# A cleared scratch row behind every gather on GpSimd, in a group convolution and deformable bottleneck for sixteen images

## The chip, the cores and the metric

The kernel runs on one core of one Trainium2 chip. The metric is the device time of one execution in microseconds (us), from the first to the last instruction and the little that lies around them. Its engines are TensorE (PE in the profile, with its weight loads as PEld), VectorE (DVE), ScalarE (ACT), GpSimd (POOL) and SyncE (SP, which only issues DMAs here).

## The reference

The input is 16 images of 512 channels and 32 x 32 pixels. `_gn` is a group norm with 32 groups of 16 channels. Two residual blocks follow each other:

```python
x = x + _L0_conv_ref(_gn(x), W, b)      # 3x3 convolution in 8 groups of 64 channels, then a
                                        # transpose of (64, 1024) to (1024, 64) read as 64 channels
x = x + _L1_conv_ref(_gn(x), ...)       # bottleneck:
    out = relu(bn(conv1x1(x)))                        # 512 -> 128 channels
    offset = conv3x3(out)                             # 18 channels: dy, dx of 9 taps
    out = deform_conv3x3(out, offset)                 # 9 taps, bilinear values at y + dy, x + dx
    out = relu(bn(conv1x1(bn(out))))                  # 128 -> 512 channels
```

A tap's value is `v00*wy0*wx0 + v01*wy0*wx1 + v10*wy1*wx0 + v11*wy1*wx1`, with `v00` to `v11` taken at four neighbouring pixels whose place depends on the data.

## The kernel before, in words

For the deformable convolution each image has a table in HBM of 1152 rows (padded pixels) of 512 float32: the 128 channels of h and of its differences in x, in y and in both. With one row of 2048 bytes a bilinear value is two multiply-adds. TensorE makes the table in nine tiles of 128 rows (`table_tile`, L868), ScalarE copies them out (L447), and SP stores them (L306). VectorE turns the offsets into row numbers `ridx` and fractions `frac` (`coordinates`, L675 to L702).

An image's deformable work is cut into 18 chunks: two halves of 512 pixels by 9 taps. A chunk is four gathers (`PER = 4`) of 128 rows each. GpSimd issues each as an indirect DMA (L335) into one of 12 row buffers, three chunks deep (`RING = 3`). VectorE waits for each gather by itself and combines its rows, first in y (L570, four a chunk), then in x (L578, four a chunk, into `val`). TensorE transposes `val` (`transpose_values`, L751), ScalarE copies the result out (L363), and TensorE multiplies it with the tap's weights (`deform`, L760). After nine chunks follow the 1x1 convolution (`out_conv`, L767), ScalarE's relu (L374), VectorE's residual (L585) and SP's store (L311).

The order of the work is written out by hand. Every engine runs the same `step` for each image, in 18 slots; in one step three images are under way at different stages, and tables of slots (`CONV_FIRST`, `SHUFFLE`, `TABLE` and so on) say what falls where. The interpolation of chunk c lies in slot c + 7, its transposes a slot later, and the product two slots later. So chunks 11 to 17 of an image are interpolated in slots 0 to 6 of the next step. The other work of TensorE is the group convolution (L778), the shuffle products (L792), the 1x1 convolution into the bottleneck (L846) and the offset convolution (L811), all for later images; in the last two steps these fall away.

GpSimd's program has a loop of its own, without slots. For each image it waits for the coordinates and the table's stores. Then for each chunk c it waits for `val_done` of chunk c - 3, which frees the row buffers (L329), and issues two gathers. Before the third it waits for `valT_done` of chunk c - 3, the transposes on TensorE (L333); this is the tie that the change's title speaks of. No buffer needs it, since the first wait has freed the rows. GpSimd's only other work is four casts of weights at the start (L344).

Of the kernel before, what the change touches and what calls it, by code (L numbers as in the profile page):

```python
# [5 lines left out]
def build_program(nc, x, w_group, b_group, w_in, w_off, b_off, w_def, w_out, bn, eye, fold, blocks, offset_fold,  # L6
# [16 lines left out]
    f32, f16, i32, u32 = mybir.dt.float32, mybir.dt.float16, mybir.dt.int32, mybir.dt.uint32  # L23
# [19 lines left out]
    CHUNKS = 2 * TAPS  # L43
# [2 lines left out]
    RING = 3  # L46
    TBUFS = 3
    PER = 4
    ROW = 4 * CH
    COLS = PIX // GIN  # L50
    XBUFS = 4
# [3 lines left out]
    with ctx:  # L55
        def sb(name, shape, dt):
            return ctx.enter_context(nc.sbuf_tensor("sb_" + name, shape, dt))

        def sem(name):
            return ctx.enter_context(nc.semaphore(name))  # L60
# [9 lines left out]
        h_split = sb("h_split", [128, 2, HPLANE], f16)  # L70
        table_sb = sb("table_sb", [128, TBUFS, ROW], f32)
        rows = sb("rows", [128, RING * PER, ROW], f32)
        val = sb("val", [128, 2, PER * CH], f32)
        valT = sb("valT", [128, 2, HALF], f32)
# [13 lines left out]
        bias_off = sb("bias_off", [128, 1], f32)  # L88
        eps_sb = sb("eps_sb", [128, 1], f32)
        warm = sb("warm", [128, 2], f32)  # L90
        bn_sb = sb("bn_sb", [128, 6, 5], f32)
        bn_s = sb("bn_s", [128, 6], f32)
        bn_t = sb("bn_t", [128, 6], f32)
# [36 lines left out]
        wo_in = sem("wo_in")  # L130
        consts_in = sem("consts_in")
        pool_passed = sem("pool_passed")
        dve_passed = sem("dve_passed")
        zeroed = sem("zeroed")
        table_loaded = sem("table_loaded")
# [43 lines left out]
        pos_done = sem("pos_done")  # L179
        gathered = [[sem(f"gathered{n}_{i}") for i in range(PER)] for n in range(RING)]  # L180
        lerp_y = sem("lerp_y")
# [13 lines left out]
        def count(per, image, n):  # L195

            total = image * per + n
            return max(total, 0) if isinstance(image, int) else total
# [119 lines left out]
        @block.gpsimd  # L318
        def _(pool):
            def step(t, u, tail, b, a2, a1):  # L320
                if not b:
                    return
                pool.wait_ge(pos_done, count(1, t, 1))
                for n in range(TBUFS):
                    pool.wait_ge(tile_stored[n], count(16 * TILES // TBUFS, t, 16 * TILES // TBUFS))
                for c in range(CHUNKS):
                    half, k = divmod(c, TAPS)

                    pool.wait_ge(val_done, count(CHUNKS, t, c - RING + 1))  # L329
                    pool.sem_inc(pool_passed, 1)  # L330
                    for i in range(PER):
                        if i == 2:
                            pool.wait_ge(valT_done, count(CHUNKS, t, c - 2))  # L333
                            pool.sem_inc(pool_passed, 1)
                        pool.indirect_dma_start(  # L335
                            out=rows[:, (c % RING) * PER + i, :], out_offset=None, in_=tables[u % 2],
                            in_offset=bass.IndirectOffsetOnAxis(
                                ap=ridx[:, u % 2, half * PER + i, k:k + 1].bitcast(u32), axis=0),
                        ).then_inc(gathered[c % RING][i], 16)


            for g in range(POOL_GROUPS, GROUPS):
                pool.wait_ge(wg_in[g // 2], 2 * 16)
                nc.gpsimd.tensor_copy(wg[:, g, :, 0:GIN], raw_wg[:, g * TAPS * GIN:(g + 1) * TAPS * GIN]  # L344
                                      .rearrange("p (k o) -> p k o", o=GIN)).then_inc(w_high, 1)

            run(pool, step)
# [640 lines left out]
```

## Time and profile before

| what | value |
|---|---|
| median of 3 runs | 2096.07 us (2092.15 to 2115.77) |
| the profiled execution | 2095.71 us |
| its span, first to last instruction | 2093.9 us |
| mean granted TensorE clock | 0.911 of full speed |
| gathers | 1152, 302.06 MB in 92160 packets |
| moved by all DMA queues | 412.98 MB, mean 197 GB/s |

The profile comes from the execution in the second line; its rows are times within the span. An engine's idle time in a row is that just before the instructions named, with what ended it: another engine, a DMA, "remote" (a releaser that the trace doesn't name) or "issue" (nothing that the profile shows).

### The profile page before, as it was taken

To read this page: it belongs to the slowest core of one execution; us is meant where nothing else is said; L and a number is where in the kernel's file an instruction comes from. 1 tells how busy PE (TensorE), PEld (TensorE's weight loads), DVE (VectorE), ACT (ScalarE), POOL (GpSimd) and SP (SyncE) were. 2 spreads that over 40 slices of the span, in tenths; PEclk is the share of its full clock that TensorE was granted. 3 is DMA by queue.
4 is the path that set the end of the run, shared out by engine and by line. 5 is a ranking of instruction groups with operands and counts; after the bars stand their busy time and mean duration, and the time that the engine had idled before them with its cause. 6 is when DMAs were issued, how large, how long until landed. Compare 5 with 4: busy or idle time off the path is not lost.

```text
span 2093.9 us, 32210 instructions
## 1 busy us (share of the span) xinstructions
PE 1759.4 (84%) x10144; PEld 975.4 (47%) x10144; DVE 1398.5 (67%) x3450; ACT 963.4 (46%) x1475; POOL 1201.4 (57%) x1160
## 2 busy tenths in 40 slices
PE   4988898988898898889889888889888889987545
PEld 2545454544545454455545444444454545444322
DVE  5447587575677758577776856758576776757654
ACT  6545454353553545454454545435454544523212
POOL 0036566555665656566566656557555556657673
PEclk9989899998999989999999999889999999999766
DMA  6055657566675756667576666657666566565764
GB/s 194 1 176 161 206 176 245 171 202 208 210 235 162 251 185 215 221 209 231 163 243 197 211 213 202 213 159 227 200 213 223 172 228 195 178 214 182 241 208 147
DMA packets 142937, 412.98 MB, mean 197 GB/s; under 512 B 24614, under 2 KB 25126, under 8 KB 142758
## 3 DMA queue, kind: packets, MB, share of 16 engines
q0 software_dynamic: 92160, 302.06, 48.1%
q1 hardware_dynamic: 50598, 108.71, 14.0%
q8 instruction: 90, 1.47, 0.3%
q14 instruction: 89, 0.73, 0.1%
HBM read 339.37 MB, written 71.30 MB: 196 GB/s over the span
## 4 chain that ended last, share of the span: by engine, by line
PE 41%; DVE 21%; another core or an unknown queue 15%; issue 12%; ACT 6%; POOL 2%; DMA 1%; SPq 1%; ACTq 0%; DVEq 0%; POOLq 0%
PE bank L778 12%; DVE sb_rows L570 8%; PE bank L760 7%; PE bank L792 6%; DVE sb_val L578 5%; PE bank L767 3%; DVE sb_split L611 3%; PE bank L751 3%; PE bank L868 3%; PE bank L846 3%; PE bank L811 2%; POOL sb_rows L335 2%; DVE sb_raw L626 2%; ACT sb_split L409 1%
## 5 line engine op out<-in xcount | busy, mean ns | idle before, releaser
L335 POOL DMA_INDIRECT sb_rows<-table,sb_ridx x1152 | 1197.0, 1039 | 851.9 <-issue 425.6
L778 PE MATMUL bank<-sb_split,sb_wg 128*128 128x512 f16 x2304 | 583.5, 400 | 43.5 <-ACT sb_conv_sb L381 31.5
L570 DVE SCALAR_TENSOR_TENSOR sb_rows<-sb_rows,sb_frac 128x256 f32<-128x256 f32 x1152 | 491.3, 479 | 107.6 <-DMA sb_rows<-table,sb_ridx 82.9
L778 PEld LDWEIGHTS bank<-sb_split,sb_wg 128*128 128x128 f16 x2304 | 225.5, 101 | 356.3 <-issue 127.5
L619 DVE TENSOR_TENSOR sb_xs<-bank,sb_xs 128x512 f32<-128x512 f32 x128 | 88.3, 690 | 416.6 <-remote 309.1
L578 DVE SCALAR_TENSOR_TENSOR sb_val<-sb_rows,sb_frac 128x128 f32<-128x128 f32 x1152 | 328.7, 347 | 54.3 <-PE bank L751 30.7
L792 PE MATMUL bank<-sb_fold_sb,sb_conv_sb 128*64 128x64 f32 x4096 | 291.8, 286 | 83.5 <-issue 69.6
L760 PE MATMUL bank<-sb_valT,sb_wd 128*128 128x512 f32 x576 | 349.0, 690 | 10.7 <-issue 9.6
L363 ACT ACTIVATE sb_valT<-bank 128x512 f32<-128x512 f32 x288 | 171.4, 595 | 362.1 <-remote 199.6
L381 ACT ACTIVATE sb_conv_sb<-bank,sb_bias 128x512 f32<-128x512 f32 x256 | 173.7, 686 | 321.1 <-PE bank L778 188.5
L792 PEld LDWEIGHTS bank<-sb_fold_sb,sb_conv_sb 128*64 128x64 f32 x4096 | 262.6, 206 | 124.2 <-issue 107.3
L751 PE MATMUL bank<-sb_eye_sb,sb_val 128*128 128x128 f32 x1152 | 193.2, 290 | 78.5 <-issue 35.6
L751 PEld LDWEIGHTS bank<-sb_eye_sb,sb_val 128*128 128x128 f32 x1152 | 147.2, 150 | 200.6 <-issue 117.6
L767 PE MATMUL bank<-sb_mid,sb_w 128*128 128x512 f32 x256 | 152.5, 681 | 41.1 <-ACT sb_res L374 27.1
L447 ACT ACTIVATE sb_table_sb<-bank 128x512 f32<-128x512 f32 x144 | 86.4, 601 | 213.6 <-PE bank L868 128.9
L611 DVE TENSOR_TENSOR sb_split<-sb_norm,sb_split 64x1024 f16<-64x1024 f32 x128 | 157.1, 1227 | 14.7 <-ACT sb_split L409 10.8
L409 ACT ACTIVATE sb_split<-sb_xs,sb_gs 64x1024 f16<-64x1024 f32 x128 | 158.1, 1236 | 1.7
L396 ACT ACTIVATE sb_norm<-sb_xs 128x1024 f32<-128x1024 f32 x128 | 134.8, 1053 | 3.9 <-DMA sb_xs<-x 2.4
L760 PEld LDWEIGHTS bank<-sb_valT,sb_wd 128*128 128x128 f32 x576 | 104.6, 209 | 53.3 <-issue 32.2
L585 DVE TENSOR_TENSOR sb_res<-sb_res,sb_xs 128x512 f32<-128x512 f32 x128 | 88.1, 689 | 49.0 <-issue 30.2
L846 PE MATMUL bank<-sb_xs,sb_w_norm 128*128 128x512 f32 x256 | 117.8, 603 | 1.1 <-ACT sb_w_norm L425 1.1
L767 PEld LDWEIGHTS bank<-sb_mid,sb_w 128*128 128x128 f32 x256 | 51.7, 212 | 124.4 <-issue 80.8
(77 smaller groups left out, 1092.4 us busy)
## 6 DMA issues: line engine op xcount, KB each, us to landing
table<-sb_table_sb SPq DMA_DIRECT2D x144, 256.0 KB
sb_xs<-x SPq DMA_DIRECT2D x64, 512.0 KB
out<-sb_res SPq DMA_DIRECT2D x128, 256.0 KB
sb_rows<-table,sb_ridx POOLq DMA_INDIRECT x1152
sb_rows<-w_group SPq DMA_DIRECT2D x8, 288.0 KB, 9.4
sb_wd<-w_def SPq DMA_DIRECT2D x1, 576.0 KB
sb_w<-w_in SPq DMA_DIRECT2D x1, 256.0 KB
sb_w<-w_out SPq DMA_DIRECT2D x1, 256.0 KB
```

The source lines that it names most:

```text
L335: pool.indirect_dma_start(out=rows[:, (c % RING) * PER + i, :], out_offset=None, in_=tables[u % 2], in_offset=bass.IndirectOffsetOnAxis(ap ...
L381: nc.scalar.activation(conv_sb[:, g % 3, half * HALF:(half + 1) * HALF], pair_ps[half][:, :], ACT.Identity, bias=bias0[:, g:g + 1]).then_i ...
L409: nc.scalar.activation(plane(split1[p, 2 * q + e, :], 1, 1, HEIGHT), xs[p, un, q, :].rearrange("p (r c) -> p r c", c=WIDTH), ACT.Identity, ...
L570: op = nc.vector.scalar_tensor_tensor(r[:, 0:2 * CH], r[:, 2 * CH:4 * CH], frac[:, parity, half * PER + i, k, 0:1], r[:, 0:2 * CH], ALU.mu ...
L578: op = nc.vector.scalar_tensor_tensor(val[:, c % 2, i * CH:(i + 1) * CH], r[:, CH:2 * CH], frac[:, parity, half * PER + i, k, 1:2], r[:, 0 ...
L611: nc.vector.tensor_tensor(plane(split1[o, 2 * q + e, :], 1, 1, HEIGHT), norm1[p, :].rearrange("p (r c) -> p r c", c=WIDTH), plane(split1[p ...
L751: op = nc.tensor.transpose(valT_ps[:, i * CH:(i + 1) * CH], val[:, c % 2, i * CH:(i + 1) * CH], eye_sb[:, :])
L760: nc.tensor.matmul(def_ps[:, :], wd[:, k * CH:(k + 1) * CH], valT[:, c % 2, :], start=k == 0, stop=k == TAPS - 1).then_inc(def_done, 1)
L767: nc.tensor.matmul(out_ps[:, :], w2[:, q * 128:(q + 1) * 128], mid[:, :], start=True, stop=True)\
L778: op = nc.tensor.matmul(pair_ps[half][:, :], wg[:, g, k, :], plane(split1[:, g, :], ky + half * HROWS, kx, HROWS), start=k == 0, stop=k == ...
L792: op = nc.tensor.matmul(shuf_ps[half][64 * e:64 * e + 64, jj * GIN:(jj + 1) * GIN], conv_sb[:, (2 * q + e) % 3, j:j + COLS * (GIN - 1) + 1 ...
L846: op = nc.tensor.matmul(pair_ps[half][:, :], w1_norm[:, q * CH:(q + 1) * CH], xs[:, (u + 1) % XBUFS, q, half * HALF:(half + 1) * HALF], st ...
```

## The change

GpSimd gets a scratch tile `spacer` of four rows of 240 float16 in each partition, which nothing reads. Behind each gather it clears one row. Before a chunk's first gather it waits until the four clears of the chunk before are done. The wait before the third gather stays.

```diff
+    SPACE = 240
...
+        spacer = sb("spacer", [128, PER, SPACE], f16)
...
+        spaced = sem("spaced")
...
                     pool.wait_ge(val_done, count(CHUNKS, t, c - RING + 1))
                     pool.sem_inc(pool_passed, 1)
+                    pool.wait_ge(spaced, count(PER * CHUNKS, t, PER * c))
+                    pool.sem_inc(pool_passed, 1)
                     for i in range(PER):
                         if i == 2:
                             pool.wait_ge(valT_done, count(CHUNKS, t, c - 2))
...
                         ).then_inc(gathered[c % RING][i], 16)
+                        nc.gpsimd.memset(spacer[:, i, :], 0.0).then_inc(spaced, 1)
```

## Rows read from the trace of the kernel before

**Rows 1.** The page, busy us (share of the span) and instructions of each engine.
```profile
PE 1759.4 (84%) x10144; PEld 975.4 (47%) x10144; DVE 1398.5 (67%) x3450; ACT 963.4 (46%) x1475; POOL 1201.4 (57%) x1160
```

**Rows 2.** Timeline of VectorE, first interpolations of images 1 and 14: start, us.
```profile
263.55 1.66 DVE L570 SCALAR_TENSOR_TENSOR sb_rows<-sb_rows,sb_frac 128x256 f32<-128x256 f32 x4
...
1869.03 1.27 DVE L570 SCALAR_TENSOR_TENSOR sb_rows<-sb_rows,sb_frac 128x256 f32<-128x256 f32 x3
```

**Rows 3.** Windows of images: us, then PE, PEld, DVE, ACT, POOL busy, clock, DMA, GB/s.
```profile
883.00:1001.00 118.00, 105.68 (x623) 59.56 (x624) 85.91 (x215) 59.68 (x92) 70.65 (x70) 0.93 0.66 210
...
1247.00:1377.00 130.00, 111.39 (x642) 61.72 (x641) 86.64 (x217) 60.21 (x93) 78.53 (x75) 0.90 0.65 203
...
1869.00:1976.00 107.00, 79.05 (x404) 42.96 (x401) 72.75 (x195) 30.56 (x52) 74.15 (x69) 0.88 0.68 210
1976.00:2072.00 96.00, 48.71 (x123) 20.80 (x124) 55.23 (x144) 17.06 (x27) 67.81 (x68) 0.68 0.68 203
```

**Rows 4.** Timeline of GpSimd, second and third gather of chunk 11: start, us, idle before and releaser.
```profile
1059.99 0.95 POOL L335 DMA_INDIRECT sb_rows<-table,sb_ridx  x1 [0.30 <-issue]
1067.05 1.91 POOL L335 DMA_INDIRECT sb_rows<-table,sb_ridx  x1 [6.11 <-PE bank L751]
```

**Rows 5.** Line L335: its durations (min/median/max, ns), and its group with the mean.
```profile
L335 POOL DMA_INDIRECT sb_rows<-table,sb_ridx x1152: 943/949/6087, 125.4 to 2070.3; - x192
...
L335 POOL DMA_INDIRECT sb_rows<-table,sb_ridx x1152 | 1197.0, 1039 | 851.9 <-issue 425.6 <-PE bank L751 277.6 <-remote 105.0
```

**Rows 6.** Waits: who waited for whom, us in total, times, longest us.
```profile
POOL sb_rows L335 <- issue: 425.6, 973, 103.1
...
POOL sb_rows L335 <- PE bank L751: 277.6, 98, 7.3
...
POOL sb_rows L335 <- remote: 105.0, 47, 4.3
DVE sb_rows L570 <- DMA sb_rows<-table,sb_ridx: 82.9, 80, 3.8
...
PE bank L792 <- issue: 69.6, 114, 1.9
...
POOL sb_rows L335 <- DVE sb_val L578: 43.8, 34, 6.6
...
PE bank L751 <- issue: 35.6, 38, 5.1
```

**Rows 7.** Waits in the last image, 1976 to 2072 us.
```profile
DVE sb_rows L570 <- DMA sb_rows<-table,sb_ridx: 29.0, 31, 2.1
```

**Rows 8.** Timeline of the start: GpSimd's clears and casts, and VectorE beside.
```profile
0.24 0.10 POOL L980 MEMSET const-float32-0.0<- 128x1 f32 x1 [0.24 <-issue]
0.27 0.10 POOL L980 MEMSET const-float32-1.0<- 128x1 f32 x1
...
16.77 1.27 POOL L344 CAST sb_wg<-sb_rows 128x576 f16<-128x576 f32 x2 [16.32 <-DMA sb_rows<-w_group]
19.40 2.91 POOL L344 CAST sb_wg<-sb_rows 128x576 f16<-128x576 f32 x2 [1.36 <-DMA sb_rows<-w_group]
...
18.95 2.82 DVE L611 TENSOR_TENSOR sb_split<-sb_norm,sb_split 64x1024 f16<-64x1024 f32 x2 [2.44 <-ACT sb_split L409]
```

**Rows 9.** Timeline of VectorE and GpSimd, chunk 0 of image 0 and its release.
```profile
144.94 1.14 DVE L578 SCALAR_TENSOR_TENSOR sb_val<-sb_rows,sb_frac 128x128 f32<-128x128 f32 x4
145.99 1.28 DVE L626 BATCH_NORM_STATS2 sb_raw<-sb_xs 128x6 f32<-128x512 f32 x2
...
146.86 0.95 POOL L335 DMA_INDIRECT sb_rows<-table,sb_ridx  x1 [6.58 <-DVE sb_val L578]
```

**Rows 10.** Timeline of VectorE and TensorE, chunk 13 of image 7.
```profile
1085.87 0.55 DVE L570 SCALAR_TENSOR_TENSOR sb_rows<-sb_rows,sb_frac 128x256 f32<-128x256 f32 x1 [0.65 <-DMA sb_rows<-table,sb_ridx]
1086.45 1.14 DVE L578 SCALAR_TENSOR_TENSOR sb_val<-sb_rows,sb_frac 128x128 f32<-128x128 f32 x4
...
1096.78 0.60 PE L751 MATMUL bank<-sb_eye_sb,sb_val 128*128 128x128 f32 x4
```

## The prediction

> **What bounds the kernel now.** I read the page's busy shares first [rows 1]: TensorE 84%, VectorE 67%, GpSimd 57%. A share alone says nothing of GpSimd's room, so the stretches by image come next. There are sixteen images; VectorE starts chunk 0 of image 1 at 263.55 and of image 14 at 1869.03 us [rows 2], so thirteen images take 1605.5 us, 123.5 each. They scatter: two of the windows are 118 us and 130 us long [rows 3]. In these TensorE is busy 106 and 111 us, GpSimd 71 and 79 us. The last two images are other: in 107 us and 96 us GpSimd is busy 74 and 68 us, while TensorE falls to 79 and 49 us [rows 3], since no later image feeds it.
>
> GpSimd's busy time is not all that a gather takes. In a run of gathers one is 0.95 us long and the next begins 0.30 us later [rows 4]; the mean of all is 1.039 us, median 0.949 [rows 5]. An image of 72 gathers so takes 72 x 1.039 = 74.8 us and 72 x 0.30 = 21.9 us between them, 96.7 us. From 123.5 us that leaves 27 us of waiting: the table of waits has 277.6 us for TensorE's transposes (the tie before the third gather), 105.0 remote and 43.8 for VectorE [rows 6], 426 us over 16 images. VectorE in turn waits for gathers 82.9 us in all [rows 6], of which 29.0 us fall in the last 96 us [rows 7]. So in the middle images TensorE and what feeds it set the pace, with GpSimd at four fifths; the last image, and part of the one before, run at GpSimd's pace.
>
> **The change, part by part.** It adds 1152 clears of 240 fp16 elements in 128 partitions, and 288 waits for the clears of the chunk before. It removes and moves nothing; SP's queue, the gathers' order and the tie of the third gather are as before. A clear moves no DMA bytes.
>
> *The clear, m.* No row of before shows it beside gathers. Nearest from below: the four start-up clears of one element begin 0.03 us apart [rows 8]. Nearest from above by element: two casts of 576 elements take 1.27 us together, 1.1 ns an element [rows 8]. A clear of 240 at that rate is 0.25 us, with 0.03 of dispatch 0.285. Ends: 0.03 if it runs in a gap that is there already. 0.59 if the 0.30 gap comes twice, behind the gather and behind the clear. 0.64 if it fares as the other two casts did (2.91 us for 1152 elements beside VectorE's two-input L611, 2.53 ns an element [rows 8]). I take 0.285: clearing is element work with nothing to read, and start-up clears follow each other with hardly a gap.
>
> The Trainium skill (GPSIMD Engine Reference, 3.1 Elementwise) has simple loop bodies at 1.03 cycles an element; at the 1.2 GHz given there 240 elements would be 0.21 us, an estimate, and the cost would end some 35 us lower than mine. This trace's casts, at 1.1 ns, are slower than that.
>
> *The wait, w.* Its instruction stops GpSimd's sequencer, and the chunk's four gathers are queued behind it; VectorE's interpolation waits for these. Until now the sequencer ran ahead of the cores. Where it did stop, a gather starts late: chunk 0's last interpolation ends at 146.0 us (four of 1.14 us in all, from 144.94, less overlap; the next row starts at 145.99), and the gather it releases starts at 146.86 [rows 9]. That is 0.85 us from the releaser against 0.30 in a run, so a chunk whose gathers would have run on pays 0.55 us. Of 18 chunks an image about two already begin behind such a stop (34 waits for VectorE in 16 images [rows 6]); 16 x 0.55 = 8.8 us. Ends: nothing if the sequencer's 0.85 is hidden behind the last clear, 9.9 if all 18 pay.
>
> *Sum per image on GpSimd.* 96.7 + 72 x 0.285 + 8.8 = 96.7 + 20.5 + 8.8 = 126.0 us. The 27 us of waiting is mostly used up. The waits are not all lost slack: the longest, some 6 us before the third gather of chunk 11 [rows 4], exists because GpSimd is three chunks ahead of TensorE, and shrinks when it comes late. I leave 0.5 us of it: a floor of 126.5 us.
>
> *What covers it.* TensorE's own 118 to 130 us. In images of 118 us the floor costs 8.5, in those of 130 none; with a mean of 123.5 and half the images under it, some 3.5 on average: 13 x 3.5 = 45 us. Lateness inside an image is partly covered: at chunk 13 VectorE already waits for gathers (0.65 us at 1085.87), but TensorE takes up that chunk's values only at 1096.78, 9 us after VectorE has them at 1087.6 [rows 10]. So a delay of 5 to 8 us there harms nobody until GpSimd's whole image is longer than TensorE's. That is why the cost follows the floor and not each late gather. If that cover were gone, every image would pay 29 us.
>
> *Last two images.* Image 14 (107 us): GpSimd's 69 gathers there busy 74.2 us, 69 x 0.585 = 40.4 us of gaps and clears, 8.8 us of waits, 123.4: +16, less the lead it starts with: +15. Image 15 (96 us) has no cover: + 20.5 + 8.8 = 29.3, less some 5 us of its idle: +24. After the last gather nothing changes.
>
> Total 45 + 15 + 24 = 84 us. The profiled execution took 2095.7 us (span 2093.9), which is the median of the runs, 2096.07, within 0.4 us. Forecast **2180 us**, 4% slower. It is steep in m: once the floor is over 123.5, 0.1 us more per clear is 7 us an image. With 0.22 the floor is 122: 13 x 1.2 + 11 + 20 = +47, 2142. With 0.40 it is 134.8: 13 x 11.3 + 24 + 33 = +204, 2300. That is the likeliest case's own range.
>
> **Rivals.**
> *Dear clear.* m is 0.45 to 0.6: the gap comes twice, or VectorE holds the clear up. For: two casts that took 1.27 us took 2.91 beside L611, and VectorE is two thirds busy, mostly with two-input work [rows 1, 8]. Against: the cast reads SBUF and a clear does not. At 0.59 the floor is 96.7 + 42.5 + 8.8 = 148: 13 x 24.5 = 319, with 37 and 46 for the last two about +400: 2500. At 0.45: 138.4, 13 x 14.9 + 27 + 36 = +257: 2353. Chance 0.18.
> The Trainium skill (SBUF — State Buffer, Who interferes with whom) says that a VectorE instruction with two SBUF inputs contends with a GpSimd instruction that reads SBUF, not with one that only writes it. By that rule the casts' slowdown, which agrees with it, does not carry over and the sum stays at m = 0.285; if it failed, this rival's 2500 would be the time.
> *Cheap clear.* It runs in the existing 0.30 gap or at two elements a step, m 0.03 to 0.13, so that the change hardly spaces anything. For: 0.03 us between start-up clears [rows 8]. Against: 240 elements at the casts' rate. The floor is 107.7 to 114.9, under the shortest image: the middle is free, the last image pays 6 to 18 and the one before 0 to 6: 2102 to 2120, 2108 as its middle. Chance 0.20; three quarters of it within 1% (21 us).
> *Faster.* Gathers spread out leave the DMA engines free for short transfers, instruction fetches among them. For: TensorE idles at issue 69.6 us before the shuffle products and 35.6 before the transposes [rows 6], and gathers take 1152 x (1.039 - 0.949) = 104 us over their median [rows 5], which might be crowding. The decision is at the floor: it must lie under 118, so m under 0.16, or this gain is eaten. If half of the 105 us goes, -53, and the last image still pays 20 or so: 2063. Against: nothing in the trace ties these stalls to gathers, and m would have to be small as well. Chance 0.07.
> The forecast case (m from 0.2 to 0.42, w near 0.55) has the remaining 0.55.
>
> **How the numbers follow.** Faster by over 1%: 0.07. Within 1% (about what a measurement of this kernel can tell from no change): 0.15 from the cheap clear and 0.02 from the low edge of the forecast, 0.17. Slower by over 1%: 0.76. The range leaves out half of the dear clear above and most of the faster case below: 2085 to 2370.
>
> **What would show it.** Right: clears of 0.2 to 0.3 us by their rows, start to start of gathers inside a chunk 1.5 to 1.6 us in place of 1.25 and 0.85 us between the last clear of a chunk and the next gather; GpSimd's waits for transposes cut to a few us an image; middle images all near 126 to 130 us instead of 118 to 130; the last image near 120 us; VectorE's wait for gathers several times 82.9 us; TensorE's busy time unchanged, more idle. Wrong: clears over 0.4 or under 0.15 us, a spacing of gathers that doesn't grow by the clear's length, middle images that stay at 123.5 with GpSimd's waits shrunk by 27 us, or shorter stalls at issue on TensorE.

## The result, and the profile after

The changed kernel takes 2126.81 us (median of 4 runs, 2123.35 to 2130.43); the kernel before took 2094.11 us on the same chip (4 runs). The ratio is 1.0118, 95% interval 1.0072 to 1.0164. So it is slower, as forecast, but by 33 us and not by 84. The profiled execution took 2130.43 us. It is the slowest of the four, 0.17% over their median; its span is 34.6 us longer than that of before.

The page of the changed kernel: busy times and the chain of work that ended last.

```profile
PE 1735.0 (82%) x10144; PEld 945.4 (44%) x10144; DVE 1435.6 (67%) x3450; ACT 969.0 (46%) x1475; POOL 1604.4 (75%) x2312
...
POOL 56%; issue 34%; PE 4%; DMA 2%; DVE 1%; POOLq 1%; ACT 1%; SPq 1%; ACTq 0%; DVEq 0%
POOL sb_rows L340 40%; POOL sb_spacer L345 16%; PE bank L784 2%; PE bank L798 1%; DMA sb_rows<-table,sb_ridx 1%; DMA sb_w<-w_out 0%; PE bank L773 0%; PE bank L852 0%; DMA table<-sb_table_sb 0%; DVE sb_val L584 0%; POOLq L335 0%; SPq L280 0%; POOLq L332 0%; SPq L289 0%; POOLq L333 0%
```

GpSimd's instructions and its gaps ("issue") hold 90% of the chain. A share of 75% busy is a full engine here, since the gaps between its instructions are the rest. Beside [rows 1], GpSimd gained 403 us of busy time and TensorE lost 24 us for the same 10144 matmuls.

Three groups of the changed kernel (busy, mean ns of one | idle before, releaser), and its waits (us in total, times, longest):

```profile
L340 POOL DMA_INDIRECT sb_rows<-table,sb_ridx x1152 | 1240.6, 1077 | 481.4 <-issue 313.9
L345 POOL MEMSET sb_spacer<- 128x240 f16 x1152 | 359.8, 312 | 1.1
L798 PE MATMUL bank<-sb_fold_sb,sb_conv_sb 128*64 128x64 f32 x4096 | 265.4, 290 | 1.8 <-issue 0.8
```

```profile
DVE sb_rows L576 <- DMA sb_rows<-table,sb_ridx: 536.7, 507, 4.6
...
POOL sb_rows L340 <- POOL sb_spacer L345: 166.7, 212, 0.8
...
POOL sb_rows L340 <- PE bank L757: 0.7, 1, 0.7
```

The clear is 0.312 us. GpSimd's wait for TensorE's transposes, 277.6 us in [rows 6], is gone (0.7), and VectorE's wait for gathers went from 82.9 to 536.7 us. The shuffle products (L798, L792 before) used to lose 69.6 us at issue [rows 6]; now 0.8.

GpSimd's timeline in the changed kernel, the end of a chunk and the start of the next:

```profile
1003.64 0.95 POOL L340 DMA_INDIRECT sb_rows<-table,sb_ridx  x1 [0.16 <-issue]
1004.59 0.31 POOL L345 MEMSET sb_spacer<- 128x240 f16 x1
1005.69 0.95 POOL L340 DMA_INDIRECT sb_rows<-table,sb_ridx  x1 [0.79 <-POOL sb_spacer L345]
1006.64 0.31 POOL L345 MEMSET sb_spacer<- 128x240 f16 x1
1007.12 0.95 POOL L340 DMA_INDIRECT sb_rows<-table,sb_ridx  x1 [0.16 <-issue]
```

Inside a chunk gathers now start 1.43 us apart (1005.69 to 1007.12), 1.25 before. The clear follows its gather with no gap, and the gap behind a clear is 0.16 us where that behind a gather was 0.30 [rows 4]. So a clear of 0.31 us costs 0.31 + 0.17 - 0.30 = 0.18 us of GpSimd's time. The wait for the last clear costs 0.79 - 0.17 = 0.62 us more.

Split by the first interpolation of each image, as in [rows 2] (in the changed kernel at 133.1, 253.3, 1868.6 and 1990.9 us for images 0, 1, 14 and 15):

| stretch | before, us | after, us | difference |
|---|---|---|---|
| start to image 0 | 143.2 | 133.1 | -10.1 |
| image 0 | 120.4 | 120.2 | -0.2 |
| images 1 to 13 | 1605.5 | 1615.3 | +9.8 |
| image 14 | 106.8 | 122.3 | +15.5 |
| image 15 and the end | 118.1 | 137.6 | +19.5 |

Windows of the changed kernel (columns as in [rows 3]): images 1 to 13, then image 14.

```profile
253.00:1869.00 1616.00, 1371.56 (x8245) 756.72 (x8244) 1150.20 (x2784) 774.62 (x1180) 1307.57 (x1873) 0.95 0.68 205
...
1869.00:1991.00 122.00, 88.25 (x397) 46.28 (x396) 74.76 (x194) 31.01 (x52) 98.91 (x143) 0.77 0.66 191
```

The same stretch of the kernel before:

```profile
263.00:1869.00 1606.00, 1408.37 (x8244) 788.98 (x8243) 1119.29 (x2784) 770.01 (x1180) 971.36 (x936) 0.93 0.65 206
```

In the middle images the same matmuls take 37 us less of TensorE, at a granted clock of 0.95 in place of 0.93. The cost arrived, and with it a gain that the forecast did not have. The cleanest place to see it is the start, where both kernels have the same work ahead of them when the first gathers run. The window from 126 to 142 us, in the changed kernel and then in the kernel before:

```profile
126.00:142.00 16.00, 16.00 (x146) 10.46 (x145) 8.63 (x24) 6.19 (x12) 12.95 (x20) 1.00 0.73 252
```

```profile
126.00:142.00 16.00, 10.35 (x78) 5.80 (x75) 0.69 (x1) 2.01 (x5) 10.93 (x12) 0.70 0.82 279
```

While the kernel before issues its first twelve gathers, TensorE gets through 78 matmuls; in the changed kernel through 146. Its timeline in the kernel before: 26 of 32 shuffle products run at once, five follow after a pause of 0.95 us and the last after another of 0.94, and the products behind them run at the lower clock (nine in 4.02 us, where nine took 2.16; the granted clock is 0.50 between 134 and 142 us). Pauses between shuffle products come back in most middle images.

```profile
127.30 2.16 PE L778 MATMUL bank<-sb_split,sb_wg 128*128 128x512 f16 x9
129.29 0.28 PE L823 MATMUL bank<-sb_sums,sb_blocks_sb 128*128 128x8 f32 x2
129.51 2.03 PE L792 MATMUL bank<-sb_fold_sb,sb_conv_sb 128*64 128x64 f32 x26
132.49 0.52 PE L792 MATMUL bank<-sb_fold_sb,sb_conv_sb 128*64 128x64 f32 x5 [0.95 <-issue]
133.95 0.34 PE L792 MATMUL bank<-sb_fold_sb,sb_conv_sb 128*64 128x64 f32 x1 [0.94 <-issue]
134.23 4.02 PE L778 MATMUL bank<-sb_split,sb_wg 128*128 128x512 f16 x9
143.45 1.01 PE L778 MATMUL bank<-sb_split,sb_wg 128*128 128x512 f16 x2 [5.20 <-ACT sb_conv_sb L381]
```

The pauses at issue are 1.9 us of this window. The longer idle stretch is the last one, 5.2 us of waiting for ScalarE, and ScalarE and VectorE were waiting for TensorE. VectorE's residual add (L619, L625 after) waits in the program for the shuffle products alone. Its two starts in the kernel before, and the one in the changed kernel that belongs to the second:

```profile
129.69 0.69 DVE L619 TENSOR_TENSOR sb_xs<-bank,sb_xs 128x512 f32<-128x512 f32 x1 [5.92 <-remote]
142.56 0.69 DVE L619 TENSOR_TENSOR sb_xs<-bank,sb_xs 128x512 f32<-128x512 f32 x1 [12.17 <-remote]
```

```profile
132.50 0.69 DVE L625 TENSOR_TENSOR sb_xs<-bank,sb_xs 128x512 f32<-128x512 f32 x1 [3.58 <-PE bank L798]
```

In the kernel before TensorE's record of the last product ends at 134.3 us, and VectorE starts 8.3 us later (ScalarE's copy, L381, at 142.62). In the changed kernel the record ends at 132.3 and VectorE starts 0.2 us later. In both traces no semaphore event of TensorE comes more than 0.03 us behind its record up to the first gather. So in this window, while the close gathers run, what the other engines see of TensorE comes late. The ends of TensorE's records are modelled, and the trace doesn't tell whether TensorE finishes later than they say or only its signal is late. "Remote" stands for this in the waits of L619: 309.1 us in all before, 5.2 in the changed kernel.

Two measures of this stall are used below. One is the time from the transposes of chunk 7 to those of chunk 8, read from TensorE's timeline: 7.8 us if nothing stalls, 11.4 us on average in images 1 to 13 of the kernel before, and over 10 us in ten of these thirteen. The other is the idle time at issue before the shuffle products. Neither counts the late hand-over by itself, and the count of matmuls in the window has both in it.

### The profile page after: what moved, and what is told of

Same layout as the page of the kernel before. It is cut to its first block, busy times and chain, and to the rows that moved or that the text cites. A ratio compares the mean times of both kernels' runs of the same rounds, so it can differ in the third digit from the quotient of the medians.

```text
span 2128.5 us, 33866 instructions
## 1 busy us (share of the span) xinstructions
PE 1735.0 (82%) x10144; PEld 945.4 (44%) x10144; DVE 1435.6 (67%) x3450; ACT 969.0 (46%) x1475; POOL 1604.4 (75%) x2312
## 3 DMA queue, kind: packets, MB, share of 16 engines
q0 software_dynamic: 92160, 302.06, 49.9%
## 4 chain that ended last, share of the span: by engine, by line
POOL 56%; issue 34%; PE 4%; DMA 2%; DVE 1%; POOLq 1%; ACT 1%; SPq 1%; ACTq 0%; DVEq 0%
POOL sb_rows L340 40%; POOL sb_spacer L345 16%; PE bank L784 2%; PE bank L798 1%; DMA sb_rows<-table,sb_ridx 1%; DMA sb_w<-w_out 0%; PE bank L773 0%; PE bank L852 0%; DMA table<-sb_table_sb 0%; DVE sb_val L584 0%; POOLq L335 0%; SPq L280 0%; POOLq L332 0%; SPq L289 0%; POOLq L333 0%
## 5 line engine op out<-in xcount | busy, mean ns | idle before, releaser
L340 POOL DMA_INDIRECT sb_rows<-table,sb_ridx x1152 | 1240.6, 1077 | 481.4 <-issue 313.9
L576 DVE SCALAR_TENSOR_TENSOR sb_rows<-sb_rows,sb_frac 128x256 f32<-128x256 f32 x1152 | 527.8, 482 | 558.0 <-DMA sb_rows<-table,sb_ridx 536.7
L784 PE MATMUL bank<-sb_split,sb_wg 128*128 128x512 f16 x2304 | 575.6, 397 | 21.5 <-ACT sb_conv_sb L387 15.1
L757 PE MATMUL bank<-sb_eye_sb,sb_val 128*128 128x128 f32 x1152 | 199.2, 299 | 243.1 <-DVE sb_val L584 214.1
L345 POOL MEMSET sb_spacer<- 128x240 f16 x1152 | 359.8, 312 | 1.1
L766 PE MATMUL bank<-sb_valT,sb_wd 128*128 128x512 f32 x576 | 342.3, 679 | 0.0
L757 PEld LDWEIGHTS bank<-sb_eye_sb,sb_val 128*128 128x128 f32 x1152 | 139.2, 151 | 394.5 <-DVE sb_val L584 327.0
L387 ACT ACTIVATE sb_conv_sb<-bank,sb_bias 128x512 f32<-128x512 f32 x256 | 173.4, 684 | 233.7 <-PE bank L784 143.2
L798 PE MATMUL bank<-sb_fold_sb,sb_conv_sb 128*64 128x64 f32 x4096 | 265.4, 290 | 1.8 <-issue 0.8
L798 PEld LDWEIGHTS bank<-sb_fold_sb,sb_conv_sb 128*64 128x64 f32 x4096 | 246.4, 209 | 33.6 <-issue 32.0
L773 PE MATMUL bank<-sb_mid,sb_w 128*128 128x512 f32 x256 | 149.6, 669 | 15.0 <-ACT sb_res L380 12.9
L625 DVE TENSOR_TENSOR sb_xs<-bank,sb_xs 128x512 f32<-128x512 f32 x128 | 87.8, 686 | 40.8 <-PE bank L798 31.0
L380 ACT ACTIVATE sb_res<-bank,sb_bn_t,sb_bn_s 128x512 f32<-128x512 f32 x128 | 99.1, 774 | 7.7 <-PE bank L773 7.7
```

Source lines behind the costliest of these rows:

```text
L340: pool.indirect_dma_start(out=rows[:, (c % RING) * PER + i, :], out_offset=None, in_=tables[u % 2], in_offset=bass.IndirectOffsetOnAxis(ap ...
L345: nc.gpsimd.memset(spacer[:, i, :], 0.0).then_inc(spaced, 1)
L387: nc.scalar.activation(conv_sb[:, g % 3, half * HALF:(half + 1) * HALF], pair_ps[half][:, :], ACT.Identity, bias=bias0[:, g:g + 1]).then_i ...
L576: op = nc.vector.scalar_tensor_tensor(r[:, 0:2 * CH], r[:, 2 * CH:4 * CH], frac[:, parity, half * PER + i, k, 0:1], r[:, 0:2 * CH], ALU.mu ...
L757: op = nc.tensor.transpose(valT_ps[:, i * CH:(i + 1) * CH], val[:, c % 2, i * CH:(i + 1) * CH], eye_sb[:, :])
L766: nc.tensor.matmul(def_ps[:, :], wd[:, k * CH:(k + 1) * CH], valT[:, c % 2, :], start=k == 0, stop=k == TAPS - 1).then_inc(def_done, 1)
```

## The experiments

The kernel before ran beside each batch: 2101 us (first four), 2100 (next four), 2074 (next four), 2076 (next three) and 2079 us (last two). The batches differ by over 1%, so each ratio is against its own; intervals are 95%. The diffs are against the kernel before, or against the changed kernel where the text says so.

### The cost in the last two images

The changed kernel, with clears and waits in images 0 to 13 alone.

```diff
+                spaced_image = a1
...
+                    if spaced_image:
+                        pool.wait_ge(spaced, count(PER * CHUNKS, t, PER * c))
+                        pool.sem_inc(pool_passed, 1)
...
+                        if spaced_image:
+                            nc.gpsimd.memset(spacer[:, i, :], 0.0).then_inc(spaced, 1)
```

> The changed kernel with clears and their waits only in images 0 to 13. Theory: the change costs 15.5 us in image 14 and 19.5 us in the last (its first interpolations and span say so) and nearly nothing before. Then this kernel gives 35 us back: 2090 to 2096 us, level with the kernel before. Rival, the cost is spread over all images and the last two only show it: 2110 to 2120.

Measured: 2097.97 us, ratio 0.9986 (0.9945 to 1.0027). Image 14 takes 113.1 us and what follows 119.0, where the changed kernel had 122.3 and 137.6 (image 14 stays 6 us over the 106.8 of before, though it has no clears). The slowdown of the whole change lies in the last two images; the thirteen middle ones are, in sum, a draw (123.8 us each; 123.5 before).

### Clears, hold and their length

Three variants: the wait asks for the last clear but one, with a fifth row for it; the changed kernel with clears of 2 elements; and clears of 2 elements with 36 rows and a wait eight chunks back, which never holds.

```diff
-        spacer = sb("spacer", [128, PER, SPACE], f16)
+        spacer = sb("spacer", [128, PER + 1, SPACE], f16)
...
-                    pool.wait_ge(spaced, count(PER * CHUNKS, t, PER * c))
+                    pool.wait_ge(spaced, count(PER * CHUNKS, t, PER * c - (c > 0)))
...
-                        nc.gpsimd.memset(spacer[:, i, :], 0.0).then_inc(spaced, 1)
+                        nc.gpsimd.memset(spacer[:, (PER * c + i) % 5, :], 0.0).then_inc(spaced, 1)
```

> The changed kernel with five scratch rows instead of four, so that a chunk waits for all but the last clear of the chunk before: the clears stay, the 0.79 us gap at each chunk goes to 0.17. Both theories: GpSimd's floor falls by 17 x 0.62 = 10.5 us an image, from 123.9 to 113.4, the last two images together cost 25 us less than in the changed kernel at most. Crowding (spaced gathers leave the instruction fetch alone): TensorE's idle time at issue before the shuffle products stays under 15 us, middle images go to 117 to 120, total 2040 to 2070. Catching up (TensorE's stalls went because it waited for VectorE): that idle time comes back to 40 to 80 us, middle images at 122 to 124, total 2095 to 2110.

```diff
-    SPACE = 240
+    SPACE = 2
```

> The changed kernel with clears of 2 elements: the wait alone. A clear of about 0.10 us and a gap of 0.17 make gathers start 1.22 to 1.26 us apart, as in the kernel before, with 0.79 us at each chunk instead of 0.30. Expected: 18 x 0.5 = 9 us more of GpSimd's time in each of the last two images, floor 106 us, hidden in the middle. Total 2100 to 2110. Crowding: the stalls before the shuffle products are as before (60 us and more), since nothing is spaced. Catching up: the same here, as GpSimd has slack.

```diff
-    SPACE = 240
+    SPACE = 2
...
-        spacer = sb("spacer", [128, PER, SPACE], f16)
+        spacer = sb("spacer", [128, 36, SPACE], f16)
...
-                    pool.wait_ge(spaced, count(PER * CHUNKS, t, PER * c))
+                    pool.wait_ge(spaced, count(PER * CHUNKS, t, PER * (c - 8)))
...
-                        nc.gpsimd.memset(spacer[:, i, :], 0.0).then_inc(spaced, 1)
+                        nc.gpsimd.memset(spacer[:, (PER * c + i) % 36, :], 0.0).then_inc(spaced, 1)
```

> Clears of 2 elements behind each gather, in 36 scratch rows, and the wait for clears eight chunks back, which is always passed: the clear instructions alone, with no hold at a chunk. What is open: in the kernel before, the slot that begins with the transposes of chunk 7 takes 11 to 13.5 us in 10 of 13 middle images, because the shuffle products in it are issued one at a time 0.7 us apart; in the runs with clears it takes 7.8. Clear theory (an instruction between the gathers is what matters): the slot is 7.8 us in nearly all images, total 2040 to 2060. Hold theory (stopping GpSimd's sequencer at each chunk is what matters): the slot is 11 to 13.5 in most, total 2090 to 2105.

Measured: the fifth row gives 2043.29 us, 0.9729 (0.9647 to 0.981), and GpSimd's wait for clears falls from 166.7 to 35.7 us. The idle time at issue is 39.2 us, which neither theory had together with this total. Clears of 2 elements with the hold give 2059.78 us, 0.9823 (0.9741 to 0.9905), faster than both theories had it, with 45.2 us of that idle time. Without the hold they give 1.0043 (1.0005 to 1.0081): they run in the gap that was there, gathers stay 1.26 us apart, and chunk 7's stall stays as well (12.3 us). So a gain of 2 to 3% was hidden under the cost, and it was not in tiny clears as such.

### What takes the stall away

A hold alone: one clear of 2 elements behind a chunk's last gather, and the wait for it before the next chunk.

```diff
+                    pool.wait_ge(spaced, count(CHUNKS, t, c))
+                    pool.sem_inc(pool_passed, 1)
                     for i in range(PER):
...
+                    nc.gpsimd.memset(spacer[:, 0, :], 0.0).then_inc(spaced, 1)
```

> One clear of 2 elements a chunk, behind the fourth gather, and the wait for it before the next chunk's gathers: the hold with a quarter of the clears. Hold theory: slot of chunk 7 at 7.8 us, total 2055 to 2075. Clear theory: mostly 11 to 13.5 us, total 2095 to 2110.

Measured: 0.985 (0.9789 to 0.9912); chunk 7's slot is 7.8 us in all thirteen images, idle at issue before the shuffle products 46.5 us.

The same hold behind the second gather of a chunk:

```diff
+                        if i == 1:
+                            nc.gpsimd.memset(spacer[:, 0, :], 0.0).then_inc(spaced, 1)
```

> One clear of 2 elements a chunk, behind the second gather instead of the fourth, waited for before the next chunk's gathers. GpSimd's sequencer can issue at most two gathers ahead of the cores at a chunk, but the cores need not pause there: gathers may still run on 0.30 us apart. If it is the sequencer's running ahead that slows TensorE, the slot of chunk 7 is 7.8 us and the total 2040 to 2060, with no cost in the last image. If it is the unbroken run of gathers (nine or more before the stall, against at most four with the hold behind the fourth), the slot stays at 11 to 13.5 and the total at 2090 to 2105.

Measured: 0.9998 (0.995 to 1.0046), slot 12.8 us (the profiled execution, 2093.07 us, was the slowest of ten). The sequencer is stopped here too, but the gathers run on nearly without a break (9.1 us of waiting for the clear in all). So it takes a pause between gathers, not a wait in the program.

Fewer bytes: each gather brings 512 bytes a partition, not 2048. The kernel leaves out the rest of each row, so its outputs are other values; the instructions on the engines stay.

```diff
-                            out=rows[:, (c % RING) * PER + i, :], out_offset=None, in_=tables[u % 2],
+                            out=rows[:, (c % RING) * PER + i, 0:CH], out_offset=None, in_=tables[u % 2].rearrange("a (b c) -> (a b) c", c=CH),
```

> The kernel before with each gather fetching 512 bytes a partition instead of 2048 (a quarter of the bytes, the rest of each row is stale, so the interpolation works on other data); instructions and their order are the same, one scratch clear at the start is added. Crowding: the 69.6 us of issue idle before the shuffle products fall under 20, total 2020 to 2060. Catching up: they stay at 50 to 80 us and the total within 1% of the kernel before in the middle images; only the last image, bound by gathers, may gain a few us.

Measured: 0.9941 (0.9899 to 0.9984), slot 12.8 us. The window of the start is the reading that counts:

```profile
126.00:142.00 16.00, 11.52 (x84) 6.53 (x84) 0.69 (x1) 2.63 (x5) 11.49 (x12) 0.80 0.42 152
```

The DMA engines' share is halved, 0.42 in place of 0.82, and TensorE still gets through 84 matmuls only. The gathers' packets fall too, from 92160 to 36864. Crowding by bytes is out, and the number of packets did not matter either. Where its 0.6% come from is open.

A slower VectorE, which sends GpSimd into its releases later (a clear of 1200 elements behind each chunk on VectorE):

```diff
+                    nc.vector.memset(idle_sb[:, :], 0.0)
```

> The kernel before with a clear of 1200 float16 on VectorE behind each chunk's interpolation, some 1.1 us x 18 = 19 us an image, GpSimd's program untouched. Catching up (TensorE's stalls go when it waits for VectorE): the slot of chunk 7 is 7.8 us in most images, and the total within 1% of the kernel before although VectorE works 19 us more an image. If the stalls are tied to what GpSimd does: the slot stays at 11 to 13.5, total 2110 to 2160.

Measured: 0.9887 (0.9827 to 0.9947), slot 10.2 us, between the two theories. Work added to a busy engine made the kernel 1.1% faster; that it does so by delaying gathers is an argument and not shown.

The tie before the third gather (the text ahead of the prediction says that the title speaks of it; the title speaks of the clears), taken out of the kernel before, then out of the hold-only kernel, then out of the changed kernel:

```diff
-                        if i == 2:
-                            pool.wait_ge(valT_done, count(CHUNKS, t, c - 2))
-                            pool.sem_inc(pool_passed, 1)
```

> The kernel before without the wait for transposes before the third gather. GpSimd then waits only for free row buffers. If holding GpSimd back is what helps TensorE, this is slower than before: 2110 to 2140. If the tie does nothing for the middle images, 2080 to 2100.

> The hold behind the fourth gather without the wait for transposes before the third: runs of gathers of at most four, but up to three chunks ahead of VectorE. If breaking the runs is enough, total 2055 to 2080, far from the 2294 us of the kernel without tie and hold. If being late relative to TensorE is what the tie gives, 2150 to 2300.

> The changed kernel without the wait for transposes before the third gather. In it GpSimd hardly waits for transposes any more (0.7 us in all), so both theories: 2125 to 2140, as the changed kernel, within 1%.

Measured: 1.0945 (1.0881 to 1.1008) without tie and hold; 0.9894 (0.9825 to 0.9962) with the hold; 1.0236 (1.016 to 1.0311) in the changed kernel. The kernel without the tie was expected at 2140 us at most and took 2293.97. Its waits show a part of the 9%:

```profile
POOL sb_rows L332 <- DVE sb_val L575: 466.6, 102, 12.9
...
PE bank L789 <- issue: 138.0, 178, 1.9
```

GpSimd waits for VectorE in 102 stops of up to 12.9 us (and in 12 for the table's stores), where it had 179 shorter ones for all its releasers [rows 6], so that more gathers follow each other between two stops. The shuffle products lose 138.0 us where they lost 69.6, 68 of the 193 us that the profiled execution is longer, and the mean clock is 0.865. The rest lies in the slots of TensorE: that of chunk 13 takes 18.4 us on average (11.5 before), that of chunk 0 takes 13.8 (6.8 before). So the tie itself is a spacer. With a hold its removal costs nothing that the intervals show, and in the changed kernel it is idle (0.7 us of waiting). That last run is in effect the changed kernel on another chip, and its ratio is 1.0236 where that of the change was 1.0118: so between ratios of different batches 1% can be the chip's.

### Spacing alone

What is left is the length of the clears without the hold. Eight rows of one-byte elements take no more memory than four of float16, and with them the wait can ask for the clears of the chunk before last. A clear of 240 bytes takes as long as one of 240 float16 (315 and 312 ns).

```diff
-        spacer = sb("spacer", [128, PER, SPACE], f16)
+        spacer = sb("spacer", [128, 8, SPACE], mybir.dt.uint8)
...
-                    pool.wait_ge(spaced, count(PER * CHUNKS, t, PER * c))
+                    pool.wait_ge(spaced, count(PER * CHUNKS, t, PER * (c - 1)))
...
-                        nc.gpsimd.memset(spacer[:, i, :], 0.0).then_inc(spaced, 1)
+                        nc.gpsimd.memset(spacer[:, (PER * c + i) % 8, :], 0.0).then_inc(spaced, 1)
```

> The kernel before with a clear of 240 one-byte elements behind each gather in all images, in 8 rows, and a wait one chunk further back, which never holds GpSimd. Gathers are spaced as in the changed kernel, if a clear of bytes takes as long as one of float16, but the sequencer is not stopped at each chunk. If it is the length of the unbroken run of gathers that makes TensorE issue slowly, and spacing alone doesn't break it: the middle images stay at 122 to 124 us, chunk 7's transposes lie 11 us or more before chunk 8's, and the time is 1.00 to 1.01 of before. If spacing by 0.17 us is enough: 7.8 us between these transposes, middle images of 119 to 120 us, and 0.97 to 0.98 of before.

Measured: 1993.14 us, 0.9594 (0.9554 to 0.9635), better than either theory had it. Its clears' group, its timeline and its window of the start:

```profile
L345 POOL MEMSET sb_spacer<- 128x240 uint8 x1152 | 362.3, 315 | 0.6
```

```profile
1005.40 0.95 POOL L340 DMA_INDIRECT sb_rows<-table,sb_ridx  x1 [0.17 <-issue]
1006.35 0.31 POOL L345 MEMSET sb_spacer<- 128x240 uint8 x1
1006.83 0.95 POOL L340 DMA_INDIRECT sb_rows<-table,sb_ridx  x1 [0.17 <-issue]
```

```profile
126.00:142.00 16.00, 13.97 (x102) 7.83 (x102) 7.50 (x21) 4.88 (x10) 14.18 (x23) 0.89 0.81 266
```

The clears and the spacing of 1.43 us are those of the changed kernel; only the hold is gone. The middle images take 116.9 us (124.3 in the changed kernel), image 14 takes 110.2 (122.3), the rest 123.5 (137.6). Chunk 7's slot is 7.8 us in every image. The clears are worth 4.1% on this chip, and the wait that the change puts beside them costs more than that. The late hand-over isn't gone: VectorE's waits for a "remote" releaser at L625 are 284.3 us in all (309.1 before), though its second residual add comes 3.2 us behind TensorE's record and not 8.3.

A hold behind every eighth gather, and the hold of each chunk in images 0 to 13 alone:

```diff
+                    if c % 2 == 0:
+                        pool.wait_ge(spaced, count(CHUNKS // 2, t, c // 2))
+                        pool.sem_inc(pool_passed, 1)
...
+                    if c % 2 == 1:
+                        nc.gpsimd.memset(spacer[:, 0, :], 0.0).then_inc(spaced, 1)
```

> The kernel before with one clear of 2 elements behind the last gather of every second chunk, and the wait for it before the next chunk: GpSimd is held behind every eighth gather, where the run with one hold a chunk held it behind every fourth (0.985 of before). If runs of more than four gathers already do the harm: little gain, 0.995 to 1.00, and chunk 7's transposes 10 us or more before chunk 8's. If the harm needs runs longer than eight, the gain is kept, 0.98 to 0.985, with 7.8 us between them.

> The kernel before with one clear of 2 elements behind each chunk and the wait for it, in images 0 to 13 alone. If the hold costs the last two images what it did in the run with the hold everywhere (image 14 6 us and the last 7 us longer than before) and gives 4 us in each middle image: 0.975 to 0.98 of before, about 2050 us, middle images of 119 us, image 14 at 107 us and 118 us behind it. If the five-row clears gave something of their own beyond the hold, this run stays behind their 0.959 by more than 1%.

Measured, with a hold behind every eighth gather: 0.9916 (0.988 to 0.9953), between the two theories, though chunk 7's slot is 7.8 to 8.5 us; here a hold comes right before the gathers that used to run into it. What is left is lost elsewhere (10.6 us at chunk 13). The hold in fourteen images gives 2017.41 us, 0.9733 (0.968 to 0.9785), with the last two images as expected (106.8 and 118.7 us) and 1.4% behind the clears.

Clears of 100 elements without a hold:

```diff
-    SPACE = 240
+    SPACE = 100
```

> As the run of 240-byte clears without a hold (0.959 of before), with clears of 100 elements in place of 240. A clear of 2 took 0.117 us and one of 240 0.315 us, so this one should take 0.20 us and gathers start 1.32 us apart, where they start 1.43 us apart with 240 and 1.25 us apart with 2 elements or none. If the gain grows with the spacing: 0.97 to 0.985 of before. If any step off 1.25 us is enough: 0.955 to 0.965. If the whole length is needed: 0.99 to 1.005, with chunk 7's transposes 10 us or more before chunk 8's, as with 2 elements and no hold.

Measured: 1.0016 (0.9983 to 1.005). Gathers start 1.32 us apart:

```profile
L345 POOL MEMSET sb_spacer<- 128x100 uint8 x1152 | 228.3, 198 | 0.7
```

```profile
126.00:142.00 16.00, 7.69 (x56) 4.20 (x55) 2.96 (x6) 1.82 (x4) 11.94 (x22) 0.76 0.74 246
```

At the start TensorE stalls as in the kernel before. In the middle images chunk 7's stall is gone and one of 11.6 us sits at chunk 13 (11.5 before, 7.9 with 240 elements). So the gain does not grow evenly with the spacing: it comes between 1.32 and 1.43 us, where no run lies. It also corrects the reading above: chunk 7's stall is one of several, and one that goes alone brings nothing.

The clears without a hold, in images 0 to 13 alone:

```diff
+                    if spaced_image:
+                        pool.wait_ge(spaced, count(PER * CHUNKS, t, PER * (c - 1)))
+                        pool.sem_inc(pool_passed, 1)
```

> As the run of 240-byte clears without a hold, in images 0 to 13 alone. If the clears cost the last two images what that run's trace shows (image 14 110.2 us, behind it 123.5 us, against 106.8 and 118.1 of before) and nothing else changes, it saves 9 us: 0.953 to 0.957 of before. If the clears help TensorE in the last images too, the gain is less, 0.957 to 0.962.

Measured: 1994.41 us, 0.9606 (0.9557 to 0.9655), the same as with clears everywhere. Image 14 falls from 110.2 to 104.5 us and the rest from 123.5 to 121.2, some 8 us, of which the medians show nothing beside the scatter of the runs (1984.89 to 2001.99).

The five-row version in images 0 to 13 alone:

> Five scratch rows, and clears and waits only in images 0 to 13. The five-row kernel paid 7.5 us in the last image (125.6 us from its first interpolation to the end against 118.1 in the kernel before) and next to nothing in image 14. Expected 2043 - 7 = 2036, faster than both kernels: 2025 to 2045.

Measured: 1986.15 us (1975.5 to 1995.11), 0.9593 (0.9517 to 0.9669), 39 us below the expected range; 27 us of it go with the chip, on which the kernel before took 2074 us and not 2101. This, the clears without a hold, and those without a hold and tail are one result within their intervals, 4% under the kernel before and 5% under the changed one by the ratios.

### The runs side by side

Half-clock time is span x 2 x (1 - mean granted clock), since the clock has two levels; the mean clock stands with each profiled execution (before 0.911 over 2093.9 us, so 373 us). It is an estimate for the profiled execution, TensorE's idle stretches included.

| kernel | start to start of gathers, us | matmuls in 126:142 | idle at issue before shuffle products, us | half-clock, us | middle image, us | ratio |
|---|---|---|---|---|---|---|
| no tie | 1.25 | 84 | 138.0 | 618 | 136.1 | 1.0945 |
| before | 1.25 | 78 | 69.6 | 373 | 123.5 | 1 |
| 2 elements, no hold | 1.26 | 82 | 81.9 | 353 | 123.9 | 1.0043 |
| 100 elements, no hold | 1.32 | 56 | 60.1 | 306 | 121.5 | 1.0016 |
| hold only | 1.25, held after 4 | 56 | 46.5 | 303 | 119.1 | 0.985 |
| 240 elements, no hold | 1.43 | 102 | 36.5 | 256 | 116.9 | 0.9594 |
| the same, 14 images | 1.43 | 116 | 28.6 | 235 | 116.9 | 0.9606 |
| the change | 1.43, held after 4 | 146 | 0.8 | 345 | 124.3 | 1.0118 |

Of the 345 us of the change 152 lie in the last two images, where gathers set the pace (101 before). The count in the window scatters: the hold gave 56 there, and in the run with the hold in fourteen images, whose program is the same up to image 13, it gave 90. Only the step to 102 and more, which every run at 1.43 us shows, stands clear of that.

## Why the prediction was right and wrong

**The clear, m: the term that was mis-sized.** Forecast 0.285 us with ends of 0.03 and 0.64; the gathers' starts moved apart by 0.18 us. That is just under the 0.2 to 0.42 of the forecast's own case, and over the 0.13 at which the cheap clear ended. The clear itself is longer than I had it (0.312), but the gap behind it is 0.16 and not the 0.30 behind a gather [rows 4]. I took the casts' 1.1 ns an element [rows 8] and added a dispatch; the clears of 2, 100 and 240 elements (117, 198 and 315 ns) give 0.83 ns an element on top of some 0.115 us, of which all but 0.01 disappears in the old gap (2 elements: 1.26 against 1.25 us). The Trainium skill (GPSIMD Engine Reference, 3.1 Elementwise) has 1.03 cycles an element, 0.86 ns at its 1.2 GHz: the slope measured agrees with it, and the fixed part is not in it.

**Dear clear: did not come.** Clears take 312 ns in the median and at least, 359 at most; those beside VectorE's two-input work, more than half of all, are among the short ones (318 at most). That agrees with the Trainium skill (SBUF — State Buffer, Who interferes with whom): an instruction that only writes is not held up.

**The wait, w: right.** 0.55 us forecast in 16 chunks an image, 0.62 measured, in all 18: the gap of 0.8 us stands before 284 of the 288 chunks, and 212 of these waits are put down to the clear. That it costs was right too: without it the same clears run 5% faster (0.9594 against 1.0118, on two chips), and image 14 and the end are 26 us shorter.

**GpSimd's floor: right in kind, 3 us too high.** With the measured sizes it is 72 x (1.077 + 0.312 + 0.166) + 18 x 0.62 = 123.1 us, where I had 126.5. The middle images take 124.3, and the chain is GpSimd's. The waits for transposes were used up, as forecast. The text called the sum steep in m, and it was: set against the thirteen middle images of before one by one (118.0 to 129.5 us), a floor of 126.5 adds 45 us in all and one of 123.1 adds 18. So 27 of the 50 us by which the forecast was off come from the floor. Of m it was 7.7 us an image too high, and longer gathers and the dearer wait put some 5 of these back.

**The last two images: right.** +15.5 us in image 14 (forecast +15), +19.5 behind it (+24), and sparing them brought the ratio back to 0.9986.

**What covers it: the step that was wrong in kind.** I took TensorE's own 118 to 130 us as fixed and put the floor beside it. With the true floor that gives +18 us in the middle images; they gave +9.8, and the stretch before image 0 gave -10.1 where I had nothing. These 18 us (and 4 in the last image) are the rest of the 50. They are small because GpSimd's floor cuts the gain off: TensorE's 118 to 130 us held stalls that come with close runs of gathers, and the change removed them (the 0.8 us at issue, 37 us less busy time, the clock of 0.95). A middle image with fewer of them and with a lower floor takes 117 us, under the shortest window that I had shown [rows 3]. So the floor of 123 us binds in every image, and the same clears that were forecast as pure cost are worth 4% once the wait beside them is gone. "TensorE's busy time unchanged" stood among the signs of a right forecast; it fell by 24 us.

**The faster rival: its mechanism, with the wrong price and the wrong cause.** "Gathers spread out" was given 0.07 and half of the gathers' excess over their median as its gain. Mean gathers became longer (1.077, from 1.039 [rows 5]), so that term had the wrong sign, and the DMA engines' load is not the cause: with a quarter of the bytes the stalls stay. The stalls at issue were named there and set aside, because "nothing in the trace ties these stalls to gathers". Something did: at the start VectorE has only two residual adds between 124 and 143 us in the kernel before, the second of them 8.3 us behind TensorE's record of what it waits for, and the twelve first gathers fill just that stretch. The decision point, a floor under 118, was needed but not enough: with m at 0.18 and no hold the floor is 112 us and the kernel is 4% faster, but clears of 2 and of 100 elements without a hold have a lower floor still and gain nothing.

**What stays open.** Why TensorE issues slowly and hands over late in a close run of gathers was not found. It is not the bytes or the packets, and not the stopping of GpSimd's sequencer as such; a slower VectorE changes it in part. Nor is it shown whether it is the distance between gathers that matters or GpSimd's pace over an image: of the clears without a hold, those of 240 elements bring its floor to 112 us, near TensorE's time, and those of 100 to 104, and no other length was tried. How much of the gain is the stall and how much the clock that falls behind it was not separated: the two go together in the table. And the hold alone helps in the middle images and not clearly at the start (56 and 90 matmuls, 78 before), so that the spacing of neighbours is not the whole rule.

## What to carry to other kernels

Before an engine's pace is taken as the cover for a slower neighbour, look at its stalls "at issue", at the "remote" waits of others for what it makes, and at what the neighbour does in those microseconds; a stretch at the start where both kernels must do the same work shows it best. Delay and order are two things: a short filler instruction behind each gather gained 4% here, and a wait for that filler, which nothing needed, took all of it and more. Where scratch rows make such a wait, give them one round more, so that the wait asks for something long done, and leave the fillers out where their engine is the one that ends last.

## What the runs showed of the hardware beyond that

- In a close run of indirect gathers on GpSimd (1.25 to 1.32 us from start to start) TensorE got through 52 to 90 matmuls in the 16 us from 126 to 142; at 1.43 us through 102 to 116, and through 146 with a hold of 0.62 us after each fourth. The step lies between 1.32 and 1.43 us.
- In such a run TensorE's results reach the others late: VectorE started 8.3 us behind the record of the products that it waited for (before), 9.7 us with the hold alone and with 100 elements, 3.2 with 240 elements and 0.2 in the changed kernel. Up to the first gather no semaphore event of TensorE was more than 0.03 us behind.
- The gap behind a gather is 0.30 us if a gather follows. A clear behind it starts at once, and the gap behind the clear is 0.16 to 0.19 us, so a clear of 2 elements costs 0.01 us and one of 240 costs 0.18.
- A clear on GpSimd costs by the element and not by the byte: 240 one-byte elements 315 ns, 240 two-byte elements 312 ns.
